# A GRU and an RK4 integrator in one scan: VectorE's order, the place of y and b, and three steps moved between engines

## The reference, cut to what matters

```python
# 1. GRU: x1[t] = x[t] + h[t]
gi = x[t] @ W_ih + b_ih;  gh = h @ W_hh + b_hh
r = sigmoid(i_r + h_r); z = sigmoid(i_z + h_z); n = tanh(i_n + r * h_n)
h = (1 - z) * n + z * h
# 2. RK4 of a FitzHugh-Nagumo network, driven by x1[t]; out[t] = x1[t] + q
def derivative(q, p, drive):
    dq = q - q**3 / 3 - p + drive + tanh(q) @ coupling.T + bias
    dp = 0.08 * (q + 0.7 - 0.8 * p)
    return dq, dp
# four derivatives at q, p; q + dt/2*dq1, ...; q + dt/2*dq2, ...; q + dt*dq3, ...
q = clip(q + dt/6 * (dq1 + 2*dq2 + 2*dq3 + dq4), -20, 20)
p = clip(p + dt/6 * (dp1 + 2*dp2 + 2*dp3 + dp4), -20, 20)
```

## Time and profile before

| what | value |
|---|---|
| median of 3 runs | 1072.88 us (1070.92 to 1073.58) |
| the profiled execution, its own time | 1072.05 us |
| its span, first to last instruction | 1070.0 us |
| mean granted TensorE clock | 0.985 |
| VectorE busy | 962.5 us, 2352 instructions |
| TensorE busy (matmul) | 949.5 us, 23809 instructions |
| ScalarE busy | 570.6 us |
| GpSimd busy | 281.1 us |

### The profile page before, as it was taken

One profiled execution on the slowest core, in us unless ns is written; L12 is line 12 of the kernel. 1 busy time (PEld: TensorE's weight loads), 2 busy tenths in 40 slices (PEclk: granted clock), 3 DMA queues, 4 the chain that ended last, 5 costly groups with the idle time before them and its releaser, 6 DMA issues.

```text
span 1070.0 us, 54115 instructions
## 1 busy us (share of the span) xinstructions
PE 949.5 (89%) x23809; PEld 930.4 (87%) x23809; DVE 962.5 (90%) x2352; ACT 570.6 (53%) x1485; POOL 281.1 (26%) x390
## 2 busy tenths in 40 slices
PE   6689999999999999999999999999999999997674
PEld 6689999988998998998998899899899889997664
DVE  5669999999999999999999999999999999999987
ACT  5545555555555555555555555555555555554442
POOL 2112222222222222222222222222222222222221
PEclk9799999999999999999999999999999999999997
DMA  9001011010100101101010010100100100000000
GB/s 344 12 8 32 23 33 28 25 31 28 33 23 28 32 23 33 28 23 32 28 30 25 28 33 23 33 28 23 33 28 30 31 13 23 23 18 18 23 13 11
DMA packets 29321, 35.71 MB, mean 33 GB/s; under 512 B 3616, under 2 KB 27936, under 8 KB 28960
## 3 DMA queue, kind: packets, MB, share of 16 engines
q1 hardware_dynamic: 29088, 32.27, 9.4%
HBM read 23.87 MB, written 8.39 MB: 30 GB/s over the span
## 4 chain that ended last, share of the span: by engine, by line
DVE 67%; issue 18%; ACT 8%; PE 4%; DMA 1%; DVEq 1%; SPq 0%; POOL 0%; POOLq 0%; ACTq 0%
DVE q L544 9%; DVE y L547 7%; DVE ps_own L674 7%; DVE ps_own L544 6%; DVE th_lo L544 6%; DVE base L547 5%; DVE y_sum L544 5%; DVE ps_rk L544 3%; DVE q_raw L544 3%; ACT ps_act L447 3%; ACT th_hi L451 3%; DVE b_raw L544 2%; DVE cube L674 2%; DVE h_lo L544 2%; DVE z_part L564 2%
## 5 line engine op out<-in xcount | busy, mean ns | idle before, releaser
L279 PE MATMUL ps_rk<-th_hi,cpl_lo 128*128 128x64 f16 x4096 | 163.9, 194 | 97.4 <-ACT th_hi L451 95.6
L279 PEld LDWEIGHTS ps_rk<-th_hi,cpl_lo 128*128 128x128 f16 x4096 | 136.8, 98 | 115.6 <-issue 109.9
L319 PE MATMUL ps_gi<-xs_hi,wih_hi 128*128 128x256 f32 x728 | 215.9, 297 | 2.0 <-ACT gi L409 1.9
L319 PE MATMUL ps_gi<-xs_lo,wih_hi 128*128 128x256 f32 x728 | 206.1, 283 | 0.0
L319 PE MATMUL ps_gi<-xs_hi,wih_lo 128*128 128x256 f32 x728 | 205.7, 283 | 0.0
L447 ACT ACTIVATE ps_act<-q 128x256 f32<-128x256 f32 x256 | 98.1, 383 | 174.7 <-DVE q L544 161.6
L279 PE MATMUL ps_rk<-th_lo,cpl_hi 128*128 128x64 f16 x4096 | 163.5, 194 | 0.0
L279 PE MATMUL ps_rk<-th_hi,cpl_hi 128*128 128x64 f16 x4096 | 163.0, 194 | 0.0
L319 PEld LDWEIGHTS ps_gi<-xs_hi,wih_hi 128*128 128x128 f32 x728 | 139.5, 192 | 2.4 <-ACT gi L409 2.4
L544 DVE SCALAR_TENSOR_TENSOR th_lo<-ps_act,th_hi 128x256 f16<-128x256 f32 x256 | 107.4, 420 | 36.2 <-ACT ps_act L455 35.9
L319 PEld LDWEIGHTS ps_gi<-xs_lo,wih_hi 128*128 128x128 f32 x728 | 139.7, 192 | 0.0
(11 more groups left out here) (143 smaller groups left out, 1964.9 us busy)
## 6 DMA issues: line engine op xcount, KB each, us to landing
ring<-x_in SPq DMA_DIRECT2D x64, 128.0 KB, 2.4
out<-ring SPq DMA_DIRECT2D x64, 128.0 KB, 2.1
xs_raw<-x_in SPq DMA_DIRECT2D x60, 128.0 KB, 2.1
gi<-wih_in SPq DMA_DIRECT2D x4, 768.0 KB, 7.1
whh_raw<-whh_in SPq DMA_DIRECT2D x4, 768.0 KB, 9.8
cpl_raw<-cpl_in SPq DMA_DIRECT2D x1, 1024.0 KB, 14.8
q<-cond_in SPq DMA_DIRECT2D x1, 128.0 KB, 6.7
h<-cond_in SPq DMA_DIRECT2D x1, 128.0 KB, 6.7
```

The lines of the kernel that those rows point to most:

```text
L279: mm = nc.tensor.matmul(ps[:, m * B:(m + 1) * B], w[:, k, w_cols + m * P:w_cols + (m + 1) * P], v[:, k * B:(k + 1) * B], start=False, stop ...
L319: last = nc.tensor.matmul(ps[:, 0:CHUNK * B].rearrange("p (j b) -> p j b", j=CHUNK), w[:, k, m * P:(m + 1) * P], v[:, :, k, :], start=(r = ...
```

## The change

It has five parts. (1) VectorE's instructions are put in another order, in which another instruction mostly stands between one that writes and one that reads; `stage_cube` stands ahead of `split_tanh_lo` in stages 1 to 3, `cell_n_in` behind `stage_q(t, 0)`, `cell_h` behind `stage_q(t, 1)`. (2) y and the next b share one place in PSUM, `y_b`: `stage_y` and `stage_b` overwrite it in turn. The sum over y goes step by step into `b_sum` (`sum_b`), which takes the place of `end_y_sum` and of `total_y`; `end_b` adds q of stage 3. (3) `cell_drive` goes from VectorE to GpSimd as a plain addition; `start_e` then makes an unscaled `e1_raw`, which ScalarE scales twice: into PSUM (`seed_e1`) and into `e1` (`scale_e1`). (4) On ScalarE `gate_n` goes behind `square(t, 1)`, `gate_rz(t + 1)` from the end of the step before to behind `square(t, 0)`, `split_h_hi` behind `square(t, 2)`, `keep_b` to the end of the step before; the first part of `gates_rz` waits for the upper part of h alone. (5) GpSimd's order and waits change: `step_q` before `cell_d`, `split_x_lo` behind `cell_x1` and `split_h_lo`. The diff, without declarations of semaphores and small constants and with blank lines left out:

```diff
         b_raw = sb("b_raw", [P, KB])
-        y = sb("y", [P, 3, KB])
-        y_sum = sb("y_sum", [P, 2, KB])
-        y_total = sb("y_total", [P, KB])
+        b_sum = sb("b_sum", [P, 2, KB])
         drive = sb("drive", [P, KB])
+        e1_raw = sb("e1_raw", [P, KB])
         e1 = sb("e1", [P, KB])
...
         th, sq = ps_act[:, 0:KB], ps_act[:, KB:2 * KB]
-        b_mid, part = ps_own[:, 0:KB], ps_own[:, KB:2 * KB]
+        y_b, part = ps_own[:, 0:KB], ps_own[:, KB:2 * KB]
         start_banks = ps_gi + [ps_act] + ps_rk + [ps_n]
...
+        e1_raw_ready = sem("e1_raw_ready")
         e1_ready = sem("e1_ready")
...
                     pe.wait_ge(rz_seeded, u + 1)
-                    pe.wait_ge(h_lo_ready, u + 1)
-                product(ps_rz, 2 * K, whh_hi, whh_lo, 0, h_hi, h_lo, rz_summed, first, end)
+                    pe.wait_ge(h_hi_ready, u + 1)
+                product(ps_rz, 2 * K, whh_hi, whh_lo, 0, h_hi, h_lo, rz_summed, first, end,
+                        before_lo=lambda: pe.wait_ge(h_lo_ready, u + 1))
...
             def seed_e1(u):
-                act.wait_ge(e1_ready, u + 1)
-                nc.scalar.activation(ps_rk[0][:, 0:KB], e1[:, :], ACT.Copy).then_inc(e1_seeded, 1)
+                act.wait_ge(e1_raw_ready, u + 1)
+                nc.scalar.activation(ps_rk[0][:, 0:KB], e1_raw[:, :], ACT.Copy, scale=rk_scale[:, 0:1]).then_inc(e1_seeded, 1)
+
+            def scale_e1(u):
+                act.wait_ge(e1_raw_ready, u + 1)
+                nc.scalar.activation(e1[:, :], e1_raw[:, :], ACT.Copy, scale=rk_scale[:, 0:1]).then_inc(e1_ready, 1)
...
             seed_e1(0)
+            scale_e1(0)
+            keep_b(0)
...
                 square(t, 0)
-                keep_b(t)
-                if t == 0:
-                    gate_rz(1)
+                if more_cells:
+                    gate_rz(t + 1)
                 if more_gates:
                     seed_rz(t + 2)
-                if more_cells:
-                    gate_n(t + 1)
                 tanh(t, 1)
                 tanh_hi(t, 1)
                 square(t, 1)
+                if more_cells:
+                    gate_n(t + 1)
+                if more_pieces:
+                    store_gi(first)
                 if more_gates:
                     seed_n(t + 2)
-                if more_pieces:
-                    store_gi(first)
-                if more_cells:
-                    split_h_hi(t + 1)
                 tanh(t, 2)
                 tanh_hi(t, 2)
                 square(t, 2)
+                if more_cells:
+                    split_h_hi(t + 1)
                 if splits_x(t):
...
                     store_gi(first + 2)
-                if more_gates:
-                    gate_rz(t + 2)
-                if more_cells:
+                if more_cells:
+                    keep_b(t + 1)
                     seed_e1(t + 1)
+                    scale_e1(t + 1)
             for t in range(T):
...
                 fma(h_lo[:, :], h[:, :], scale[:, MAG_COND:MAG_COND + 1], h_hi[:, :], h_lo_ready, ALU.subtract)
-
-            def cell_drive(u):
-                dve.wait_ge(x1_ready, u + 1)
-                fma(drive[:, :].rearrange("p (k b) -> p k b", b=B), ring[:, u % SLOTS, :].rearrange("p (k b) -> p k b", b=B),
-                    rk_scale[:, 0:1], drive_bias[:, :].unsqueeze(2).broadcast_to([P, K, B]), drive_ready)
...
                 dve.wait_ge(sq_ready, 4 * t + s + 1)
+                if s == 1:
+
+                    dve.wait_ge(n_in_ready, min(t + 2, T))
                 nc.vector.scalar_tensor_tensor(out=cube[:, :] if s == 0 else part, in0=sq, scalar=-OWN[s], in1=q[:, s, :],
...
+
             def stage_y(t, s):
-
                 wait(dve, q_ready, 4 * t + s)
                 if s == 0:
                     wait(dve, b_ready, t)
-                    tt(y[:, 0, :], q[:, 0, :], b_state[:, :], ALU.subtract, y_ready)
+                    wait(dve, b_raw_ready, t)
+                    tt(y_b, q[:, 0, :], b_state[:, :], ALU.subtract, y_ready)
                 else:
                     dve.wait_ge(b_mid_ready, 2 * t + s)
-                    tt(y[:, s, :], q[:, s, :], b_mid, ALU.subtract, y_ready)
+                    tt(y_b, q[:, s, :], y_b, ALU.subtract, y_ready)
             def stage_b(t, s):
-                dve.wait_ge(y_ready, 3 * t + s + 1)
-                fma(b_mid, y[:, s, :], B_STEP, b_state[:, :], b_mid_ready)
+                dve.wait_ge(e_seeded, 3 * t + s + 1)
+                dve.wait_ge(b_sum_ready, 3 * t + s + 1)
+                fma(y_b, y_b, B_STEP, b_state[:, :], b_mid_ready)
             def seed_e(t, s):
                 dve.wait_ge(y_ready, 3 * t + s)
-                fma(ps_rk[s % 2][:, 0:KB], y[:, s - 1, :], minus_y[:, s - 1:s], e1[:, :], e_seeded)
+                dve.wait_ge(e1_ready, t + 1)
+                fma(ps_rk[s % 2][:, 0:KB], y_b, minus_y[:, s - 1:s], e1[:, :], e_seeded)
             def start_e(u):
                 dve.wait_ge(drive_ready, u + 1)
                 wait(dve, b_ready, u)
-                fma(e1[:, :], b_state[:, :], minus_b[:, 0:1], drive[:, :], e1_ready)
+                fma(e1_raw[:, :], b_state[:, :], -1.0 / BETA, drive[:, :], e1_raw_ready)
+
+            def sum_b(t, s):
+
+                dve.wait_ge(y_ready, 3 * t + s + 1)
+                if s == 0:
+                    dve.wait_ge(b_kept_ready, t + 1)
+                    fma(b_sum[:, 0, :], y_b, B_STEP / 3, b_kept[:, :], b_sum_ready)
+                elif s == 1:
+                    dve.wait_ge(b_sum_ready, 3 * t + 1)
+                    fma(b_sum[:, 1, :], y_b, 2.0 * B_STEP / 3, b_sum[:, 0, :], b_sum_ready)
+                else:
+                    dve.wait_ge(b_sum_ready, 3 * t + 2)
+                    dve.wait_ge(e_seeded, 3 * t + 3)
+                    fma(y_b, y_b, (2.0 - 2.0 * B_STEP) * B_STEP / 3, b_sum[:, 1, :], b_sum_ready)
...
-            def end_y_sum(t, i):
-                if i == 0:
-                    dve.wait_ge(y_ready, 3 * t + 2)
-                    fma(y_sum[:, 0, :], y[:, 1, :], 2.0, y[:, 0, :], y_sum_ready)
-                else:
-                    dve.wait_ge(y_ready, 3 * t + 3)
-                    dve.wait_ge(y_sum_ready, 2 * t + 1)
-                    fma(y_sum[:, 1, :], y[:, 2, :], 2.0 - 2.0 * B_STEP, y_sum[:, 0, :], y_sum_ready)
-
             def end_b(t):
-                dve.wait_ge(y_total_ready, t + 1)
-                dve.wait_ge(b_kept_ready, t + 1)
-                fma(b_raw[:, :], y_total[:, :], B_STEP / 3, b_kept[:, :], b_raw_ready)
+                dve.wait_ge(b_sum_ready, 3 * t + 3)
+                dve.wait_ge(q_ready, 4 * t + 3)
+                fma(b_raw[:, :], q[:, 3, :], B_STEP / 3, y_b, b_raw_ready)
...
             split_h_lo(0)
-            dve.wait_ge(cpl_scaling, 14)
-            cell_drive(0)
             start_e(0)
...
                 stage_y(t, 0)
-                stage_b(t, 0)
                 seed_e(t, 1)
+                sum_b(t, 0)
                 split_tanh_lo(t, 0)
                 stage_cube(t, 0)
                 if more_cells:
                     cell_n_rh(t + 1)
+                stage_b(t, 0)
+                stage_q(t, 0)
+
+                if more_cells:
                     cell_n_in(t + 1)
-                stage_q(t, 0)
-
                 stage_y(t, 1)
+                stage_cube(t, 1)
+                split_tanh_lo(t, 1)
+                seed_e(t, 2)
+                stage_base(t, 1)
+                sum_b(t, 1)
+                if more_cells:
+                    cell_z(t + 1)
                 stage_b(t, 1)
-                seed_e(t, 2)
-                split_tanh_lo(t, 1)
-                stage_cube(t, 1)
-                stage_base(t, 1)
-                if more_cells:
-                    cell_z(t + 1)
+                stage_q(t, 1)
+
+                if more_cells:
                     cell_h(t + 1)
-                stage_q(t, 1)
-
                 stage_y(t, 2)
+                stage_cube(t, 2)
+                split_tanh_lo(t, 2)
+                seed_e(t, 3)
+                stage_base(t, 2)
                 if more_cells:
                     split_h_lo(t + 1)
-                seed_e(t, 3)
-                split_tanh_lo(t, 2)
-                stage_cube(t, 2)
-                stage_base(t, 2)
-                end_y_sum(t, 0)
-                end_y_sum(t, 1)
+                sum_b(t, 2)
                 stage_q(t, 2)
                 end_q_sum(t)
-                if more_cells:
-                    cell_drive(t + 1)
+                end_b(t)
+                stage_cube(t, 3)
+                clip_b(t)
                 split_tanh_lo(t, 3)
-                stage_cube(t, 3)
                 stage_base(t, 3)
-                end_b(t)
-                clip_b(t)
                 if more_cells:
...
+            def cell_drive(u):
+                pool.wait_ge(x1_ready, u + 1)
+                add(drive[:, :].rearrange("p (k b) -> p k b", b=B), ring[:, u % SLOTS, :].rearrange("p (k b) -> p k b", b=B),
```

(65 more changed lines are left out.)

## The result

The changed kernel takes 1006.37 us (median of 4 runs, 1006.0 to 1007.58) against 1071.9 us for the kernel before on the same chip (median of 4): ratio 0.9393, 95% interval 0.937 to 0.9417, 6.1% faster. The prediction was 1019 us with a range of 1000 to 1047. The profiled execution took 1006.48 us, its span is 1004.7 us.

What follows compares the result with a forecast made beforehand. VectorE (90% busy) bounds the kernel, TensorE (89%) close behind. Saving 0.94 us in 53 steps (49.8) and 0.41 in nine (3.7) takes the span from 1070.0 to 1016.5; with 2.05 around it and the median's 0.8, 1019 us, range 1000 to 1047.

Steps and rivals of the forecast that it cites:

- stage-by-stage walk: One step followed by the starts of stage_q through stages 1, 2, 3 and 0: 14.80 us against 15.74, 0.94 less.
- four distances: From each stage_q start to the next, into stages 1, 2, 3 and 0: 4.07, 3.79, 3.42 and 3.52 us.
- The last ten steps: Without split_x_lo a step takes 15.21 us; against 14.80 that saves 0.41, over nine steps 3.7 us.
- Neighbours: On VectorE, start to start: independent neighbours 0.34 us, 0.40 with a scalar from a tile; dependent ones 0.11 to 0.12 more.
- The wait of TensorE's third part for th_lo: In a coupling, TensorE's third part was to start 0.15 us after the end of VectorE's th_lo.
- Waits: On VectorE, a late second wait costs 0.11 us after its source ends, a single or first late wait 0.04.
- Contention: VectorE instructions with two SBUF inputs are stretched while GpSimd works: b_mid 0.25, y_sum 0.51, together 0.76 us a step.
- a sign of being wrong: VectorE instructions on y_b at 0.49 us would show the forecast wrong; it priced y_b in PSUM at nothing.
- the rival of a late drive: GpSimd's cell_drive comes too late for start_e; at 4 us for the drive the run takes 1103 us; chance 0.08.
- TensorE limits stage 0: TensorE is free for stage 0's coupling 0.13 us later than clip_q would allow it to start.
- ScalarE's two scalings have hardly any cover: The scalings of e1_raw, 0.40 to 0.48 us each, free ScalarE 0.1 us before the next step's q.
- th_lo of stage 3 is late: In stage 3 clip_b stands between cube and th_lo, so TensorE's third part of the coupling waits 0.34 us.

Runs made afterwards that it cites:

- experiment 3: Kernel before with stage 1's order cube, base, z, h changed to cube, z, base, h: 1061.87 us, ratio 0.991.
- experiment 9: Changed kernel with th_lo ahead of the cube in stages 1 to 3 and th_lo's two waits exchanged, the square's first: 995.29 us, ratio 0.9295.
- experiment 2: Kernel before with GpSimd's cell_x1 moved up right behind step_q, so it no longer runs beside y_sum: 1044.49 us, ratio 0.9752.
- experiment 1: Changed kernel with y of the three stages back in SBUF, b and the last partial sum still in PSUM: 1049.23 us, ratio 0.9794.
- experiment 4: Changed kernel with cell_drive taken off GpSimd, back on VectorE as an addition between end_b and stage 3's cube: 1005.41 us, ratio 0.938.
- experiment 6: Changed kernel with the gate tanh of r and z back at the end of the step before, behind scale_e1: 1028.91 us, ratio 0.9612.
- experiment 7: Changed kernel with th_lo of stage 3 ahead of clip_b instead of behind it, nothing else: 993.62 us, ratio 0.9277.
- experiment 8: Changed kernel with th_lo ahead of the cube in stages 1 to 3, and so ahead of clip_b in stage 3: 1007.25 us, ratio 0.9398.
- 5: Changed kernel with gate_n ahead of stage 1's tanh on ScalarE and n_in ahead of stage 0's stage_q on VectorE: 1021.41 us, ratio 0.9525.
- Experiment 10: Changed kernel with stage 3's th_lo ahead of clip_b and seed_e of stages 1 and 2 ahead of the cube: 978.67 us, ratio 0.9127.

## Why the prediction was right

The sign, the mechanism and the stage-by-stage walk held. Its four distances were 4.07, 3.79, 3.42 and 3.52; measured are 4.03, 3.75, 3.32 and 3.50. The step came out at 14.60 instead of 14.80. Of the 12.6 us that the forecast was too high, 53 steps at 0.20 are 10.6, and 0.7 more are single longer steps, of which the kernel before has more (16.10 instead of 15.74, for instance). The median was to lie 0.8 above the profiled execution and lay 0.1 below it. The last ten steps saved 4.1 us, against 3.7 forecast, and that agreement is luck. The 15.21 of the earlier trace rows held for five of them only: steps 59 to 62 of the kernel before took 15.65 to 15.95 us, three of them at a granted clock of 0.80 to 0.89. The changed kernel lost to the clock there too, and its last step was 1.5 us longer than before (16.33 against 14.81). Term by term:

- Neighbours. 0.34 for an independent neighbour is 0.33 in the new order (base, z, stage_q), four to a stage: 0.04 too much in each of stages 1 and 2. A dependent one costs its 0.11 (experiment 3).
- The wait of TensorE's third part for th_lo was priced at 0.15, by th_hi's row. It measured 0.06 (513.43 to 513.49). This term was mis-sized, by 0.09 of the 0.20; what makes the two differ was not tested.
- Waits. The cube starts 1.63 to 1.64 after `stage_q`, as forecast; the old th_lo started after 1.70. The price of a late second wait was right, and experiment 9 shows that it hangs on the order of the waits.
- Contention. y_sum's 0.93 was on the path (experiment 2), and y in PSUM is what keeps seed_e out of the same (experiment 1). No instruction on y_b is above 0.49. The prediction had named 0.49 there as a sign of being wrong; only seed_e shows it, and seed_e took 0.48 to 0.49 before.
- The drive was hidden with 1.5 us to spare, so the rival of a late drive was far off. But it would have been as well hidden on VectorE (experiment 4).
- TensorE limits stage 0 by about 0.1, ScalarE's two scalings have hardly any cover, and th_lo of stage 3 is late: all three were in the prediction, and experiments 6, 7 and 8 showed each on the path.

The part that the prediction left vague is what adjacency itself gave. The stages tell: setting neighbours apart put the cube early and made it wait, and stage 1 is 0.16 longer than before. Stage 2 lost the 0.51 by which y_sum was stretched. In stage 3, start to start, `end_b` left the path for the idle time ahead of the cube (0.34), two dependent pairs were set apart (0.12 behind the cube, 0.11 behind `end_b`), e no longer stands right behind the clipped b with its late second wait (0.20), and the cube starts 0.07 sooner than th_lo did; against this, `stage_q` now waits for TensorE (0.08). That is 0.76 of the 0.78. The drive is not among these: it stood in idle time before. This is a reading of the two traces; no run undid these exchanges one by one. Undone singly, the place of y in PSUM costs 43 us (experiment 1), the place of `gate_rz` 23 (6), that of n_in and `gate_n` 15 (5), and that of the drive nothing (4). Experiment 10 puts an adjacent pair back and is faster, because the pair fills a wait.

## What to carry to other kernels

Walk the critical engine's own order instruction by instruction, with start-to-start distances for independent and for dependent neighbours, beside the order of the engine that is second; the sum by stages was within 1.4% of a step. A gap between dependent neighbours is worth removing only where it is not in front of a wait; put such pairs where the engine idles, and let the instruction that another engine waits for come first. Two-input VectorE work in SBUF beside GpSimd work is a cost to look for by comparing the same form at two places of a trace.

## What the runs showed of the hardware

The order of two waits of one VectorE instruction counts: if the late one is second, it starts 0.10 to 0.12 us after the signal's source ends (`th_lo_ahead_all`), if it is first, 0.03 to 0.04 (`late_wait_first`). The start of th_lo moved by 0.06 to 0.09 with nothing else changed.

With y in SBUF, seed_e starts 0.05 us before GpSimd's addition in the record and is the one stretched, by 0.58, while GpSimd keeps its 0.73. In the same run sum_b of stage 2 (515.32, two SBUF inputs) starts 0.16 us before GpSimd's `split_x_lo` (515.48); there VectorE keeps 0.42 and GpSimd takes 0.84 instead of 0.73. The order of the starts in the record alone does not tell which of the two is stretched.

In the last steps of the changed kernel the granted clock dips (columns as above):

```profile
910.00:924.00 14.00, 10.10 (x287) 9.91 (x284) 11.89 (x34) 7.24 (x20) 3.53 (x5) 0.88 0.08 22
925.00:939.00 14.00, 9.98 (x323) 9.58 (x319) 12.49 (x35) 6.95 (x18) 3.52 (x5) 1.00 0.08 22
```

The step that fills the first window took 15.63 us, its neighbour at 1.00 took 14.59. From 984.74 to 997 us the clock stands at 0.50, the lower of its two levels. TensorE had been busy for 14.50 of 14.59 us in step 57 and for 10.57 of 14.59 in a step at full clock after the projection had ended. But `seed_in_idle`, with 10.24 of 13.75 busy, keeps a clock of 1.00 throughout these steps. What decides between the two is not shown.
